# A router on unsplit fp32 operands, in quarters of TensorE's columns, in an expert-weighted linear layer on one core

## What is computed

```python
xc = einsum('bsi,boi->bso', x, weight[ids])             # "cond", one 1024x1024 matrix a sequence
logits = xc @ W_router.T                                # 8 experts
probs = softmax(logits); top 2, renormalised -> combine
h = einsum('nd,erd->ner', xc, A_stack) * combine        # rank 16, 8 experts: 128 rows
out = x + xc @ W_base.T + b_base + einsum('ner,eor->no', h, B_stack) * 2
```

## Time and profile before

| | us |
|---|---|
| median of 3 runs | 407.63 (407.60 to 407.68) |
| the profiled execution | 407.98 |
| its span in the trace | 406.2 |
| TensorE busy | 399.7 (98%) |
| VectorE busy | 302.5 (74%) |
| ScalarE busy | 186.3 (46%) |
| GpSimd busy | 39.9 (10%) |

### The profile page before, as it was taken

One profiled execution on the slowest core, in us unless ns is written; L12 is line 12 of the kernel. 1 busy time (PEld: TensorE's weight loads), 2 busy tenths in 40 slices (PEclk: granted clock), 3 DMA queues, 4 the chain that ended last, 5 costly groups with the idle time before them and its releaser, 6 DMA issues.

```text
span 406.2 us, 5339 instructions
## 1 busy us (share of the span) xinstructions
PE 399.7 (98%) x2008; PEld 338.7 (83%) x2008; DVE 302.5 (74%) x432; ACT 186.3 (46%) x286; POOL 39.9 (10%) x67
## 2 busy tenths in 40 slices
PE   7999999999999999999999999999999999999996
PEld 6788888888888888888888888888888888888885
DVE  3888947789799999764547697478868999987322
ACT  4776834758633345221145686257666233441000
POOL 0101100101000130011162000000000003001110
PEclk9999999999999999999999999999999999999999
DMA  6999780778430056376569878146184003621222
GB/s 228 361 322 318 295 329 24 249 247 284 156 103 2 27 181 208 129 242 224 194 216 368 298 246 302 61 148 224 44 266 142 7 21 103 200 94 76 79 79 77
DMA packets 21210, 72.84 MB, mean 179 GB/s; under 512 B 2832, under 2 KB 2848, under 8 KB 21184
## 3 DMA queue, kind: packets, MB, share of 16 engines
q1 hardware_dynamic: 15984, 56.11, 40.1%
q0 software_dynamic: 4912, 15.87, 11.1%
q10 hardware_dynamic: 288, 0.52, 0.4%
HBM read 64.10 MB, written 8.39 MB: 178 GB/s over the span
## 4 chain that ended last, share of the span: by engine, by line
PE 96%; DMA 1%; SPq 1%; DVE 0%; issue 0%; ACT 0%
PE bank_x L801 29%; PE bank_x L805 15%; PE bank_y L786 9%; PE bank_y L787 9%; PE bank_y L788 9%; PE bank_x L786 8%; PE bank_x L787 8%; PE bank_x L788 8%; PE bank_y L844 2%; PE bank_y L845 2%; DMA raw<-w_cond 1%; PE bank_y L868 0%; SPq L357 0%; SPq L341 0%; PE bank_y L860 0%; DVE out_sb L590 0%
## 5 line engine op out<-in xcount | busy, mean ns | idle before, releaser
L801 PE MATMUL bank_x<-x_hl,wc_hl 128*128 128x512 f32 x512 | 128.8, 393 | 2.1 <-ACT wc_hl L488 2.1
L466 ACT CAST wc_hl<-raw 128x1024 fp32r<-128x1024 f32 x90 | 94.0, 1051 | 69.4 <-PE bank_y L788 34.8
L539 DVE TENSOR_TENSOR wc_hl<-raw,wc_hl 128x1024 fp32r<-128x1024 f32 x90 | 108.7, 1220 | 23.0 <-ACT wc_hl L466 22.9
L801 PEld LDWEIGHTS bank_x<-x_hl,wc_hl 128*128 128x128 f32 x512 | 92.1, 189 | 18.9 <-ACT wc_hl L488 2.5
L805 PEld LDWEIGHTS bank_x<-x_hl,wc_hl 128*128 128x128 f32 x512 | 70.1, 190 | 5.2
L805 PE MATMUL bank_x<-x_hl,wc_hl 128*128 128x256 f32 x512 | 71.7, 282 | 0.0
L582 DVE SCALAR_TENSOR_TENSOR out_sb<-bank_x,bias_sb,out_sb 128x512 f32<-128x512 f32 x32 | 23.7, 747 | 24.6 <-PE bank_x L788 19.1
L418 POOL DMA_DIRECT2D out<-out_sb x28 | 15.3, 545 | 257.7 <-DVE out_sb L590 236.1
L786 PE MATMUL bank_x<-x_hl,wc_hl 128*128 128x512 f32 x96 | 37.4, 389 | 0.0
L788 PE MATMUL bank_x<-x_hl,wc_hl 128*128 128x512 f32 x96 | 37.4, 389 | 0.0
L787 PE MATMUL bank_x<-x_hl,wc_hl 128*128 128x512 f32 x96 | 37.3, 389 | 0.0
(11 more groups left out here) (94 smaller groups left out, 507.7 us busy)
## 6 DMA issues: line engine op xcount, KB each, us to landing
raw<-w_cond SPq DMA_DIRECT2D x62, 512.0 KB, 5.3
raw<-w_base SPq DMA_DIRECT2D x24, 512.0 KB, 5.0
out_sb<-x POOLq DMA_DIRECT2D x32, 256.0 KB, 5.5
raw<-x SPq DMA_DIRECT2D x15, 512.0 KB, 5.1
out<-out_sb POOLq DMA_DIRECT2D x28, 256.0 KB, 2.3
raw<-w_cond SPq DMA_DIRECT2D x4, 256.0 KB, 4.8
out<-out_sb SPq DMA_DIRECT2D x4, 256.0 KB, 2.0
raw<-x ACTq DMA_DIRECT2D x2, 256.0 KB, 2.8
```

The source lines that it names most:

```text
L466: nc.scalar.copy(split_dst(key, HI), split_src(key)).then_inc(hi_done, 1)
L539: nc.vector.tensor_tensor(split_dst(key, LO), split_src(key), split_dst(key, HI).bitcast(F32), ALU.subtract).then_inc(lo_done, 1)
L801: nc.tensor.matmul(ps[:], wc_hl[:, slot_of(s, t), HI, k], x_hl[:, s % 2, k].rearrange("p h n -> p (h n)"), start=(k == 0), stop=False)
```

## The change

The router's operands aren't split any more. `router(p)` has 8 matmuls, one for each k, of plain fp32: the moving operand is `xp` (fp32, 128 x 512), the weights are 32 columns of `wr_sb` (8 experts, then 24 zeros). Step k is placed in quarter `j = k % 4` of the array's columns and writes partitions 32j to 32j+31 of `ps_logit`, so that each quarter adds up two of the eight steps, and the bank holds four partial sums of each logit. ACT copies all 128 rows; the four transposes become full ones of 128 x 128; DVE adds the four partial sums where it added two.

With that go the clearing of `wr_hl`, ACT's cast and DVE's split of the weights, and three semaphores. The load of the weights has 128 KB instead of 32 KB. The router waits for sums (`xc_summed`) instead of low parts; `lora_down` has the waits for low parts.

```diff
-NR = 2 * EXPERTS
+CG = 4
+NR = P // CG
...
-        logit_t = gate_er[0:NR].rearrange("p q e r -> p (q e r)")
+        logit_t = gate_er[:].rearrange("p q e r -> p (q e r)")
...
-        tok_parts = ps_tok[:, 0:NQ * NR].rearrange("p (q n) -> p q n", q=NQ)
+        tok_parts = ps_tok[:].rearrange("p (q j n) -> p q n j", q=NQ, j=CG)[:, :, 0:EXPERTS]
...
-                nc.scalar.copy(logit_t, ps_logit[0:NR, :]).then_inc(logit_copied, 1)
+                nc.scalar.copy(logit_t, ps_logit[:]).then_inc(logit_copied, 1)
...
-                        if (s, t) == (1, 0):
-                            act.wait_ge(wr_in, 16)
-                            act.wait_ge(wr_clear, 1)
-                            nc.scalar.copy(wr_k[:, :, 0:EXPERTS], wr_raw[:]).then_inc(wr_hi, 1)
...
-            nc.vector.memset(wr_hl[:].bitcast(F32), 0.0).then_inc(wr_clear, 1)
...
-                chain(nc.vector.tensor_reduce(logit[:], tok_parts.rearrange("p q (h e) -> p q e h", h=2), AX.X,
-                                              ALU.add))
+                chain(nc.vector.tensor_reduce(logit[:], tok_parts, AX.X, ALU.add))
...
             def router(p):
+
                 if p == 0:
-                    pe.wait_ge(wr_split, 1)
+                    pe.wait_ge(wr_in, 16)
                 if p == 2:
                     pe.wait_ge(pass_done, passed(0, "C12", HT - 1))
                 for k in range(KT):
-                    if k == 0 or k == KT - 1:
-                        pe.wait_ge(xc_lo, p * (2 * KT) + KT + (KT - 1 if k == 0 else KT))
-                    w = wr_hl[:, k * NR:k * NR + P]
-                    nc.tensor.matmul(ps_logit[:], w, xc_hl[:, k, HI], start=(k == 0), stop=False)
-                    mm = nc.tensor.matmul(ps_logit[:], w, xc_hl[:, k, LO], start=False, stop=(k == KT - 1))
+                    if k == 0 or k >= KT - 2:
+                        pe.wait_ge(xc_summed, p * (2 * KT) + KT + (KT - 2 if k == 0 else k + 1))
+                    j = k % CG
+                    mm = nc.tensor.matmul(ps_logit[j * NR:(j + 1) * NR, :], wr_sb[:, k], xp[:, p % 2, k],
+                                          start=k < CG, stop=k >= CG, tile_position=(0, j * NR))
                 mm.then_inc(router_done, 1)
 
             def lora_down(p):
                 if p == 0:
                     pe.wait_ge(lo_done, SPLIT["a", 0, 0])
                 for k in range(KT):
+                    if k == 0 or k >= KT - 2:
+                        pe.wait_ge(xc_lo, p * (2 * KT) + KT + (KT - 2 if k == 0 else k + 1))
...
-                            tok = nc.tensor.transpose(tok_parts[:, q], logit_t[:, q * P:(q + 1) * P],
-                                                      ident[0:NR, 0:NR])
+                            tok = nc.tensor.transpose(ps_tok[:, q * P:(q + 1) * P], logit_t[:, q * P:(q + 1) * P],
+                                                      ident)
```

More of the change, by code:

```diff
@@ L215, in build @@
         b_hl = sb("b_hl", [P, 2, KT + HT, P], F32R)
-        wr_raw = sb("wr_raw", [P, KT, EXPERTS])
-        wr_hl = sb("wr_hl", [P, (KT - 1) * NR + P], F32R)
-        wr_k = wr_hl[:, 0:KT * NR].rearrange("p (k n) -> p k n", n=NR)
+        wr_sb = sb("wr_sb", [P, KT, NR])
         bias_sb = sb("bias_sb", [P, KT])
@@ L257, in build @@
         summed = sem("summed")
-        wr_clear = sem("wr_clear")
-        wr_hi = sem("wr_hi")
-        wr_split = sem("wr_split")
         cond_done = sem("cond_done")
@@ L402, in _ @@
             pool.wait_ge(cond_done, 3)
-            nc.gpsimd.dma_start(wr_raw[:], w_router).then_inc(wr_in, 16)
+            nc.gpsimd.dma_start(wr_sb[:], w_router).then_inc(wr_in, 16)
             nc.gpsimd.dma_start(const_sb[:], consts).then_inc(consts_in, 16)
@@ L678, in _ @@
                         c = s * KT + t + 1
[L679 to L683, removed]
                         xc = xp[:, s // 2 % 2, t, s % 2 * TOK:(s % 2 + 1) * TOK]
@@ L958 @@
     b_t = np.asarray(L0_ffn_B_stack).transpose(0, 2, 1)
+    wr_t = np.zeros((P, KT, NR), np.float32)
+    wr_t[:, :, 0:EXPERTS] = np.asarray(L0_ffn_W_router).reshape(EXPERTS, KT, P).transpose(2, 1, 0)
     arrays = {
@@ L963 @@
         "w_base": wb_t.reshape(2, 2, P, 2, D),
-        "w_router": np.asarray(L0_ffn_W_router).reshape(EXPERTS, KT, P).transpose(2, 1, 0),
+        "w_router": wr_t,
         "lora_a": a_t.reshape(P, D),
```

## The result

The changed kernel takes 402.56 us (median of 4 runs, 402.38 to 402.73) beside 407.65 us (407.60 to 407.98) of the kernel before: a ratio of 0.9868, 95% interval 0.9856 to 0.9881. So it is 5.1 us faster, where 2.2 us slower was forecast. The profiled execution took 402.67 us with a span of 400.9, against 407.98 and 406.2: 5.3 us less in the trace.

A forecast was written before the change was run, and what follows sets the result against it. TensorE's queue, busy 98% of the span, was taken as the bound. Four routers of 4.14 + 0.20 us make 17.36, less 14.77 removed, less 0.4 for transposes: +2.2, so 409.8 us; range 400.8 to 417.5.

The forecast's parts named there:

- ACT's copy of the second pair's logits: Logits' copy on ACT: ends at 112.90, TensorE asks for it at 113.0 if quarters run side by side, just covered.
- the staircase: Router: only one matmul's second part and the next one's first run together; 4.14 us a router, total 409.8, chance 0.37.
- 18 slots: Router: nine parts of two slots each, 4.14 us; a slot is a 512-column pass with its weight load, 0.23 us.
- the rival's 8 slots: Router: four fp32 matmuls start together, two rounds of four 0.23 us passes, 1.84 us before any wait.
- The rival, 401.6 us: Router: four quarters truly side by side, a matmul not holding back the next; -6.0 us, chance 0.33.
- Routers up to the end of their last part: Four routers side by side, each ending 0.92 us after DVE's last sum: 2.40 + 3 x 1.98 = 8.34 us.
- The shape: Entering and leaving the quarters around each router: 0.20 us added a router, with 0 and 0.40 as ends.
- The transposes: After the router: full transposes take 0.44 us without excess for 0.34 + 0.20, 0.10 less a pair, 0.4 in all.
- the side-by-side case without a cost for the shape: Router: four quarters at once, nothing added for changing the array's shape; 400.8 us.
- One by one: Router: each pass queues separately, only last and next first overlap; 25 slots, 5.75 us, +8.6, 416.2 us, chance 0.11.
- not at all: Router: the quarters don't overlap; 32 slots, 7.36 us, +15.1, total 422.7 us, chance 0.13.
- cheaper than four slots: Router: a side-by-side fp32 matmul costs under four 0.23 us passes, last sum's wait sets it; -8.8, 398.8 us, chance 0.05.

The follow-up runs named there:

- the kernel with pairs: The changed kernel with k = 0, 1 in quarter 0, k = 2, 3 in quarter 1 and so on; 402.82 us.

## Why the prediction was wrong

**The bound was right.** TensorE's queue set the time, the clock never fell, no new wait came up in P1 to P5, and ACT's copy of the second pair's logits, covered by 0.1 us in the forecast, was started at 110.64 and held `lora_down` up by 0.04 us (a step of 0.27 instead of 0.23); the fourth pair's did the same.

**The step that failed** is the choice of the staircase, "order in the queue is what the rows show and independent quarters are what they don't show". The two halves of its premise came out differently. That an fp32 matmul is two parts with their own weights, and four passes in all, was right (64 records, 6.98 us in one quarter). That the second part of k = 0 holds back k = 1 was wrong. The rows behind it show matmuls that all use the whole array and start 0.23 us apart; they say nothing about matmuls that need different quarters. The run with neighbours in the same quarter shows that the engine starts a matmul 13 ns after the first even with another one for the busy quarter ahead of it. With it fell the forecast's 18 slots, 4.14 us a router: measured were four parts of 0.43 us, 1.72 us, which is the rival's 8 slots, and with the wait for the sum and the change of shape 2.16 us.

**The rival, 401.6 us, was the case that came true.** Term by term, with its number first:
- Routers up to the end of their last part: 8.34 us, with the last sum 1.48 us (first pair) and 1.06 us (others) after the start. Measured: 4 x 2.07 = 8.28. The last sum ended 1.14 us after the first load in every pair and k = 7 started at 1.19; its second part followed after 0.45 us. That the total fits to 0.06 us is partly luck: the first pair's 1.48 was 0.34 us too high, and the other three's 1.06 was 0.08 too low each.
- The shape: 0.20 us a pair, measured 0.30 (0.10 in, 0.20 out). That is 0.4 us more in all; the upper end that I gave for this term, 0.40 a pair, takes it in.
- The transposes: 0.10 a pair, measured 0.10.
- Not foreseen: +0.27 us in each of the two stretches of block products, +0.54 us; and some 0.2 us in the steps of `lora_down` after the router, of which 0.08 is the wait for the copy in the second and fourth pair.
- The start of the program was 0.3 us shorter in this trace, which differs from run to run (4.8 to 5.6 us from the first warm-up matmul to the first real one in three traces of the changed kernel).

In sum 8.28 + 1.2 - 14.77 - 0.4 + 0.54 + 0.2 - 0.3 = -5.25, and the trace is 5.3 us shorter. The wait of k = 7, which the rival priced, is real, and moving the router behind six matmuls takes it away.

**The range and the chances.** 402.56 lies in the range, which took in everything from the side-by-side case without a cost for the shape (400.8) to 417.5, but on the side with the smaller chance: faster had 0.38, slower 0.50. *One by one* and *not at all* are refuted by the two-quarter and four-quarter kernels; *cheaper than four slots* by the one with one quarter.

**What was priced right beside it**: the removed split and clearing of the weights gave nothing that stands out of the scatter of the program's start, TensorE never waited for the longer load of 128 KB, and the longer copy (579 ns) and reduction (288 ns) stayed hidden but for the 0.04 us above.

## What to carry to other kernels

Rows in which every instruction needs the whole of a resource can't tell how instructions that need parts of it would queue. When the size of a change hangs on that, a forecast should say so, and not let the order in those rows decide. For a thin product of 32 output rows or less (8 are used here), unsplit fp32 in four quarters costs one pass of the array a step (1.72 us for eight steps, 0.215 each, four passes and four steps at once), where a single fp32r matmul took 0.23, and saves the splitting; count 0.3 us for each visit to the quarters, keep the visit in one piece, and put work of the full array ahead of it that covers the last operand.

## What the runs showed of the hardware

- A plain fp32 matmul of 512 columns leaves two matmul records and two weight loads, 429 ns from one to the next at the full clock (453 ns after the first part of a visit to a quarter, 434 in the whole array), whether it has 32 weight columns in a quarter or 128 in the whole array.
- Matmuls in different quarters start 7 ns apart and run together. A matmul waiting for its quarter, or the second part of one, doesn't keep later ones for free quarters from starting (13 ns apart with one passed over). The order isn't one that was fixed beforehand, if the same eight calls were lowered alike: k = 7's first load comes behind the second loads of k = 4 to 6 where its sum is late (1188 ns after 886 to 900), and ahead of them where it isn't (477 ns).
- The Trainium skill, page TensorE: Matmul & The Clock Gate, Part 3: Packing small matmuls — row/col tiling, says that matmuls start and end in program order. For the whole array the rows agree. With quarters the measured starts differ: in the kernel with pairs the first part of k = 6 starts at 42 ns, and no second part of any matmul before 455 ns.
- Entering the quarters costs 0.10 us and leaving them 0.20 us; leaving the 16-row transposes costs about the same 0.20 us, which the full transposes don't.
